# A fused graph-network kernel: the dense second layer with its residual folded into the weights, its sum copied by ScalarE and its roots taken by ScalarE and VectorE

## The chip, the cores and the metric

The kernel runs on one core of one Trainium2 chip. The metric is the device time of one execution in microseconds. The engines are TensorE (PE for its matmuls, PEld for its weight loads), VectorE (DVE), ScalarE (ACT), GpSimd (POOL) and SyncE (SP), which issues the large DMAs.

## The reference

Four graph-network layers run one after the other over the same 50,000 nodes of 128 features and 12,500 edges. Each is followed by a residual and a normalisation per row. The layer that matters here is the second (L1):

```python
def _L1_gnn_ref(x, edge_index, W):
    deg = jax.ops.segment_sum(ones(E), row, num_segments=n_nodes)
    inv_sqrt = jax.lax.rsqrt(deg + 1.0)
    xs = x * inv_sqrt[:, None]
    agg = jax.ops.segment_sum(xs[col], row, num_segments=n_nodes) + xs
    out = agg * inv_sqrt[:, None]
    return jnp.matmul(out, W.T)
# around it: x2 = normalise(x1 + L1(x1)), with mean and variance over the 128 features of a row
# normalise(v) = (v - mean(v)) / sqrt(var(v) + 1e-5)
```

A node without an edge has degree 0, so for it the layer is just `x1 @ W.T`, and its new row is `normalise(x1 @ W.T + x1)`.

## The kernel before

The kernel is one program of stages that follow each other, with a barrier between them. `second_layer()` is the stage that changes. It does two things side by side:

- **The dense part** treats all nodes as if they had no edge. The nodes are cut into 98 groups (`NG`) of 512 rows, each held as a tile of 128 x 512 (four blocks of 128 x 128, `spans`). Two groups form a pair `d` (49 pairs, `NPR`), which shares the small operations on 8 numbers per partition.
- **The edge part** computes the rows of nodes that do have edges, in 25 groups (`EGR`) of 512 edges, from rows gathered by GpSimd's indirect DMAs. Later stages take these rows where they exist.

For a dense group g the work is: `load_dense` (SP brings x1 into `dx_flat[g % 6]`), `dense_turn` (TensorE transposes it into PSUM `DT`, which is one buffer), `dense_copy` (ScalarE copies `DT` to `dxT[g % 2]`), `dense_output` (TensorE multiplies by `WL1` into `DY[g % 2]`), `dense_residual` (VectorE adds x1 and writes `dr_flat[g % 6]`), `dense_stats` and `dense_moments` (VectorE, mean and variance). Per pair follow `dense_eps` (VectorE adds 1e-5 to 8 variances), `dense_power` (GpSimd raises them to -0.5), `dense_shift` (VectorE), and then per group `dense_normalise` (ScalarE, four activations with a scale and a bias per partition) and `store_dense`.

For an edge group the work is `gather_peer` and `gather_own` (GpSimd), `scale_peer` (VectorE, L2461), `turn_peer` (TensorE, L2359), `scale_own` (ScalarE, L2409), `turn_own` (TensorE), `segment_sums`, `add_own` (VectorE), `output` (TensorE), `residual`, `stats`, `moments`, `eps` (VectorE), `power` (GpSimd), `shift` (VectorE) and `normalise` (ScalarE, L2417).

The order on each engine is written out by hand. Each engine runs a loop over k, where one turn of k (a step, from here on) takes one edge group and four dense groups. An engine executes its instructions strictly in this order and waits on semaphores (`after(engine, semaphore, g)` waits until event g has happened). TensorE's step is:

```python
for k in range(EGR + 1):
    dense(2 * k)                      # turn(4k), output(4k-1), turn(4k+1), output(4k)
    staged(k, EGR, turn_peer)
    staged(k - 1, EGR, turn_own)
    dense(2 * k + 1)                  # turn(4k+2), output(4k+1), turn(4k+3), output(4k+2)
    staged(k - 1, EGR, output)
```

So the dense groups that come after `turn_peer` in this order wait for the peer's scaled rows, whether they need them or not.

## Time and profile before

| what | value |
|---|---|
| median of 3 runs | 4410.17 us (4407.81 to 4410.22) |
| the profiled execution's own time | 4406.22 us |
| its span in the trace | 4404.2 us |
| `second_layer` in the trace | about 1439 to 1835 us |
| busy in that stretch of 396 us | DVE 335.6, POOL 308.8, ACT 273.8, PE 240.0 us |
| granted TensorE clock there | 0.80 of full |
| DMA | 0.67 of the 16 engines, 197 GB/s |

The stage is 9% of the span, and the change touches nothing outside it. "Busy" is the time in which an engine has an instruction running. An engine with a high busy share is not necessarily the one that sets the time. For this the waits are needed. A granted clock of 0.50 is TensorE's lower level, 1.2 GHz, and 1.00 the upper one, 2.4 GHz.

### The profile page before, as it was taken

Reading aid. Unit: us, or ns where it says so; the run is one execution under the profiler, and the core shown is the slowest. Engines: PE = TensorE matmul, PEld = TensorE weight load, DVE = VectorE, ACT = ScalarE, POOL = GpSimd, SP = SyncE. Lnnn points to the kernel's source line nnn. Section 1 sums busy time; section 2 is a strip of 40 time slices with the busy share of each in tenths; the row PEclk is TensorE's granted clock in tenths of the full one; section 3 lists DMA queues with packets and bytes.
Section 4 is the critical chain, followed back from the end, with each engine's and each line's share of the span. In section 5 each row is a group of like instructions: output and inputs, shape, how many; then the busy total and the mean of one; then the engine's idle time right before and its main releaser. Section 6 shows DMA issues by size and latency. Waiting matters only on the chain. (4 is left out here: it accounts for less than half of the span.)

```text
span 4404.2 us, 59487 instructions
## 1 busy us (share of the span) xinstructions
PE 3497.0 (79%) x14981; PEld 2181.8 (50%) x14981; DVE 3360.6 (76%) x10477; ACT 2304.7 (52%) x4672; POOL 3043.6 (69%) x2666
## 2 busy tenths in 40 slices
PE   5688888747776566499979999999699678687984
PEld 3466666624444566444435555555344367564331
DVE  6888888846666788655647888888688689787985
ACT  2498888713344577523337777777233222132752
POOL 1378888757775788677737888888577567463547
PEclk9999999979999788799989999999899889898997
DMA  3254445433332677444433443443344278694873
GB/s 86 92 146 140 138 142 148 124 98 91 96 96 75 187 203 207 143 131 143 137 116 105 133 132 125 133 132 116 106 129 133 77 233 253 142 194 132 278 235 119
DMA packets 463646, 621.80 MB, mean 141 GB/s; under 512 B 71541, under 2 KB 220204, under 8 KB 463308
## 3 DMA queue, kind: packets, MB, share of 16 engines
q1 hardware_dynamic: 402700, 534.09, 38.6%
q0 software_dynamic: 54912, 83.37, 9.0%
q8 instruction: 125, 2.05, 0.2%
q14 instruction: 213, 1.74, 0.1%
q10 hardware_dynamic: 5696, 0.55, 0.1%
HBM read 402.95 MB, written 218.46 MB: 141 GB/s over the span
## 5 line engine op out<-in xcount | busy, mean ns | idle before, releaser
L1195 PE MATMUL ps<-big,Whh 128*128 128x512 f32 x1176 | 537.4, 593 | 0.5 <-ACT big L1400 0.5
L1615 PE MATMUL ps<-big,We 128*128 128x512 f32 x800 | 355.5, 598 | 8.4 <-DVE big L1765 4.5
L1195 PEld LDWEIGHTS ps<-big,Whh 128*128 128x128 f32 x1176 | 212.9, 191 | 214.2 <-issue 211.4
L1228 POOL TENSOR_TENSOR big<-big 128x512 f32<-128x512 f32 x196 | 248.0, 1285 | 71.5 <-ACT big L1222 71.5
L604 POOL DMA_INDIRECT me<-node_tab,ix x208 | 239.7, 1152 | 70.8 <-issue 48.3
L611 POOL DMA_INDIRECT meta<-me,rank_ix x208 | 223.4, 1074 | 63.1 <-issue 60.5
L1765 DVE SCALAR_TENSOR_TENSOR big<-r2N,zN 128x512 f32<-128x512 f32 x400 | 254.0, 686 | 9.9 <-ACT zN L1676 6.2
L1213 DVE SCALAR_TENSOR_TENSOR big<-ps,bhh,hid 128x512 f32<-128x512 f32 x196 | 146.4, 747 | 141.2 <-ACT hid L1206 137.4
L1615 PEld LDWEIGHTS ps<-big,We 128*128 128x128 f32 x800 | 150.8, 191 | 195.1 <-issue 188.7
L688 PE MATMUL ps<-big,hotrow 128*128 128x256 f32 x832 | 201.5, 398 | 22.5 <-ACT hotrow L746 12.1
L1238 POOL TENSOR_TENSOR big<-big 128x512 f32<-128x512 f32 x98 | 141.5, 1464 | 109.1 <-DVE big L1233 109.1
L2729 POOL DMA_INDIRECT xN<-x_tab,ix x100 | 167.1, 1671 | 62.1 <-PE ps L2743 30.1
L1205 ACT ACTIVATE hid<-ps,brz 128x512 f32<-128x512 f32 x196 | 134.8, 688 | 135.2 <-PE ps L1195 129.9
L700 PE MATMUL ps<-agg,W2a 128*128 128x512 f32 x392 | 193.4, 617 | 8.8 <-ACT hid L724 4.6
L688 PEld LDWEIGHTS ps<-big,hotrow 128*128 128x128 f32 x832 | 164.7, 201 | 61.0 <-issue 23.5
L637 POOL TENSOR_TENSOR rsq<-veq,mhalf 128x4 f32<-128x4 f32 x98 | 104.6, 1067 | 127.5 <-DVE veq L921 125.6
L2759 PEld LDWEIGHTS ps<-big,hid 128*128 128x128 f32 x1600 | 186.1, 194 | 8.7 <-DVE hid L2878 3.5
L2759 PE MATMUL ps<-big,hid 128*128 128x128 f32 x1600 | 188.8, 277 | 1.2 <-DVE hid L2878 1.2
L1704 ACT ACTIVATE win<-hid 128x512 f32<-128x512 f32 x50 | 31.5, 630 | 294.6 <-DVE hid L1783 294.6
L2729 POOL DMA_INDIRECT xN<-d_tab,ix x100 | 141.0, 1410 | 64.0 <-PE ps L2743 36.1
L2806 ACT ACTIVATE big<-ps 128x512 f32<-128x512 f32 x50 | 29.9, 597 | 288.6 <-PE ps L2759 288.6
L2431 ACT ACTIVATE hid<-big,shq,rsq 128x128 f32<-128x128 f32 x392 | 160.4, 482 | 32.7 <-DVE shq L2538 32.6
(421 smaller groups left out, 11045.9 us busy)
## 6 DMA issues: line engine op xcount, KB each, us to landing
xN<-x_tab SPq DMA_DIRECT2D x196, 256.0 KB, 3.3
h_tab<-yN SPq DMA_DIRECT2D x124, 256.0 KB, 2.4
krow<-key_row SPq DMA_DIRECT2D x100, 256.5 KB, 4.4
agg<-in_xt SPq DMA_DIRECT2D x98, 256.0 KB, 3.3
big<-x_tab SPq DMA_DIRECT2D x98, 256.0 KB, 3.1
x_tab<-hid SPq DMA_DIRECT2D x98, 256.0 KB, 3.5
agg<-x_tab SPq DMA_DIRECT2D x98, 256.0 KB, 2.8
x_tab<-zN SPq DMA_DIRECT2D x98, 256.0 KB, 2.0
```

Source lines behind the costliest of these rows:

```text
L604: nc.gpsimd.indirect_dma_start(me[:, t, f:f + 4], None, node_tab, at_index(which, i, j)).then_inc(noted[i % 2].sem, 16)
L611: nc.gpsimd.indirect_dma_start(meta[k], bass.IndirectOffsetOnAxis(ap=rank_ix[:, k, t:t + 1], axis=0), me[:, t, :], None).then_inc(stored[k ...
L688: last = nc.tensor.matmul(LOOK[j // 2][:, (j % 2) * LO:(j % 2 + 1) * LO], hotrow[k][:, h, j * P:(j + 1) * P], R[:, k, h, :], start=(h == 0 ...
L700: nc.tensor.matmul(HB[h][:, :], W2a[:, 0, h * P:(h + 1) * P], xt[g % 4], start=True, stop=True).then_inc(hidd, 1)
L1195: last = nc.tensor.matmul(bank[:, :], Whh[:, l, c * D:(c + 1) * D], h, start=True, stop=not both)
L1213: nc.vector.scalar_tensor_tensor(self.n[u], A[u][:, :], bhh[:, self.l, 2:3], self.rz[u][:, 0, :], ADD, MUL).then_inc(first, 1)
L1228: nc.gpsimd.tensor_tensor(self.d[u], h[u], self.n[u], SUB).then_inc(self.dd, 1)
L1615: last = nc.tensor.matmul(MS[:, :], We[:, l * NTYPE + t, :], masked[g % 2][:, t, :], start=(t == 0), stop=(t == NTYPE - 1))
L1765: last = nc.vector.scalar_tensor_tensor(masked[u][:, t, :], types[u], float(t), hs[u], EQ, MUL)
L2431: last = nc.scalar.activation(dx2_flat[g % 8][:, spans[j]], dr_flat[g % 6][:, spans[j]], ACT.Identity, scale=rsq[d % 2][:, c:c + 1], bias= ...
L2729: nc.gpsimd.indirect_dma_start(xg[u][:, j, :], None, x3_tab if l == 0 else d1_tab, at_index(IX_SRC if l == 0 else IX_SLOT, g + EDGE0, j)). ...
L2759: last = nc.tensor.matmul(OUT[u][:, spans[j]], ranked[u][m][:, spans[j]], weightI[l][m], start=(m == 0), stop=(m == TOP - 1))
```

## The change

Four things are done in `second_layer()`:

1. `with_own = WL1 + identity` is built once by VectorE in a free buffer. `dense_output` multiplies by it, so the product already holds x1 @ W.T + x1.
2. `dense_residual` on VectorE goes. `dense_evict` on ScalarE copies `DY` to `dr_flat`.
3. `dense_power` on GpSimd goes. `dense_root` on ScalarE takes the square root of the 8 values of a pair, and `dense_inverse` on VectorE takes the reciprocal and refines it with one Newton step: four small operations, each waiting for the one before it.
4. `load_dense(g)` waits for the transposes of group g - 6 and no longer for its residual, since x1's tile is not read after the transposes.

The diff:

```diff
@@ -2247,6 +2247,7 @@
             ph = Phase()
             (same_d, scale_d, peer_t, scan_d, own_d, own_t, sum_d, out_d, res_d, st_d, mv_d, eps_d, rstd_d, shift_d, x2_d) = ph.sems(15)
             dt_d, dc_d, dy_d, dr_d, ds_d, dm_d, de_d, dp_d, dh_d, dx_d = ph.sems(10)
+            root_d, guess_d, square_d, error_d, mixed = ph.sems(5)
             keys_in, x2_out, dense_in, dense_out = ph.sems(2), ph.sems(2), ph.sems(6), ph.sems(8)
             peer_in, own_in = gat_a, gat_b
             per = 16 * J
@@ -2267,6 +2268,9 @@
             dx2_flat = [hid2[q][u][:, h, :] for q in range(2) for u in range(2) for h in range(2)]
             d_stats = norm_bufs[1][0]
             NPR = NG // 2
+            with_own = hotrow[0][:, 1, 0:P]
+            d_root = [hotrow[0][:, 0, 8 * u:8 * u + 8] for u in range(2)]
+            d_error = [hotrow[1][:, 0, 8 * u:8 * u + 8] for u in range(2)]
 
             def both(t):
                 return t[:, :].rearrange("p (a j) -> p a j", a=2)
@@ -2293,7 +2297,7 @@
                         sp.dma_start(x2_rows(1, g + EDGE0), x2[g % 2][:, :, :]).then_inc(x2_out[g % 2], 16)
 
                     def load_dense(g):
-                        after(sp, dr_d, g - 6)
+                        after(sp, dt_d, g - 6)
                         sp.dma_start(dx_flat[g % 6], group(x1_tab, g)).then_inc(dense_in[g % 6], 16)
 
                     def store_dense(g):
@@ -2336,19 +2340,11 @@
                         after(pool, eps_d, g)
                         nc.gpsimd.tensor_tensor(rs[g % 2][:, :, 0], ve[g % 2][:, :, 0], mhalf[:, 0:J], ALU.pow).then_inc(rstd_d, 1)
 
-                    def dense_power(d):
-                        after(pool, de_d, d)
-                        after(pool, dh_d, d - 2)
-                        after(pool, dx_d, 2 * (d - 2) + 1)
-                        nc.gpsimd.tensor_tensor(rsq[d % 2][:, :], veq[d % 2][:, :], mhalf[:, 0:2 * J], ALU.pow).then_inc(dp_d, 1)
-
                     gather_peer(0)
                     for k in range(EGR + 4):
                         staged(k + 1, EGR, gather_peer)
-                        staged(2 * k - 1, NPR, dense_power)
                         staged(k, EGR, gather_own)
                         staged(k - 2, EGR, power)
-                        staged(2 * k, NPR, dense_power)
 
                 @block.tensor
                 def _(pe):
@@ -2381,10 +2377,12 @@
                         last.then_inc(dt_d, 1)
 
                     def dense_output(g):
+                        if g == 0:
+                            pe.wait_ge(mixed, 1)
                         after(pe, dc_d, g)
                         after(pe, dr_d, g - 2)
                         for j in range(J):
-                            last = nc.tensor.matmul(DY[g % 2][:, spans[j]], dxT[g % 2][:, spans[j]], WL1[:, :], start=True, stop=True)
+                            last = nc.tensor.matmul(DY[g % 2][:, spans[j]], dxT[g % 2][:, spans[j]], with_own, start=True, stop=True)
                         last.then_inc(dy_d, 1)
 
                     def dense(d):
@@ -2422,6 +2420,16 @@
                         after(act, dy_d, g - 2)
                         nc.scalar.activation(dxT[g % 2], DT[:, :], ACT.Copy).then_inc(dc_d, 1)
 
+                    def dense_evict(g):
+                        after(act, dy_d, g)
+                        after(act, dx_d, g - 6)
+                        nc.scalar.activation(dr_flat[g % 6], DY[g % 2][:, :], ACT.Copy).then_inc(dr_d, 1)
+
+                    def dense_root(d):
+                        after(act, de_d, d)
+                        after(act, guess_d, d - 2)
+                        nc.scalar.activation(d_root[d % 2], veq[d % 2][:, :], ACT.Sqrt).then_inc(root_d, 1)
+
                     def dense_normalise(g):
                         d, a = divmod(g, 2)
                         after(act, dh_d, d)
@@ -2435,7 +2443,9 @@
                     def dense(d):
                         for n in range(2):
                             staged(2 * d + n, NG, dense_copy)
+                            staged(2 * d + n - 1, NG, dense_evict)
                             staged(2 * (d - 2) + n, NG, dense_normalise)
+                        staged(d - 1, NPR, dense_root)
 
                     for k in range(EGR + 3):
                         staged(k - 1, EGR, scale_own)
@@ -2445,6 +2455,7 @@
 
                 @block.vector
                 def _(dve):
+                    nc.vector.tensor_tensor(with_own, WL1[:, :], ident[:, :], ADD).then_inc(mixed, 1)
                     nc.vector.memset(agg[1][:, 0, :], 0.0).then_inc(scan_d, 1)
 
                     def same_key(g):
@@ -2507,11 +2518,6 @@
                         after(dve, x2_d, g - 2)
                         nc.vector.scalar_tensor_tensor(sh[u][:, :, 0], mv[u][:, :, 0], -1.0, rs[u][:, :, 0], MUL, MUL).then_inc(shift_d, 1)
 
-                    def dense_residual(g):
-                        after(dve, dy_d, g)
-                        after(dve, dx_d, g - 6)
-                        nc.vector.tensor_tensor(dr_flat[g % 6], DY[g % 2][:, :], dx_flat[g % 6], ADD).then_inc(dr_d, 1)
-
                     def dense_stats(g):
                         after(dve, dr_d, g)
                         after(dve, dm_d, g - 2)
@@ -2532,20 +2538,32 @@
                         after(dve, dp_d, d - 2)
                         nc.vector.tensor_scalar(both(veq[d % 2]), moment(d)[:, :, :, 1], EPS, None, ADD).then_inc(de_d, 1)
 
+                    def dense_inverse(d):
+                        y, t, v = rsq[d % 2][:, :], d_error[d % 2], veq[d % 2][:, :]
+                        after(dve, root_d, d)
+                        after(dve, dh_d, d - 2)
+                        after(dve, dx_d, 2 * (d - 2) + 1)
+                        nc.vector.reciprocal(y, d_root[d % 2]).then_inc(guess_d, 1)
+                        after(dve, guess_d, d)
+                        nc.vector.tensor_tensor(t, y, y, MUL).then_inc(square_d, 1)
+                        after(dve, square_d, d)
+                        nc.vector.scalar_tensor_tensor(t, t, -0.5, v, MUL, MUL).then_inc(error_d, 1)
+                        after(dve, error_d, d)
+                        nc.vector.scalar_tensor_tensor(y, t, 1.5, y, ADD, MUL).then_inc(dp_d, 1)
+
                     def dense_shift(d):
                         after(dve, dp_d, d)
                         after(dve, dx_d, 2 * (d - 2) + 1)
                         nc.vector.scalar_tensor_tensor(both(shq[d % 2]), moment(d)[:, :, :, 0], -1.0, both(rsq[d % 2]), MUL, MUL).then_inc(dh_d, 1)
 
                     def dense_second(d):
+                        staged(d - 2, NPR, dense_inverse)
                         staged(d - 2, NPR, dense_shift)
-                        staged(2 * d - 1, NG, dense_residual)
                         staged(2 * d - 1, NG, dense_stats)
                         staged(2 * d - 1, NG, dense_moments)
                         staged(d - 1, NPR, dense_eps)
 
                     def dense_first(d):
-                        staged(2 * d, NG, dense_residual)
                         staged(2 * d, NG, dense_stats)
                         staged(2 * d, NG, dense_moments)
```

The order in which two engines now run a step, from the steady part of the stage. On ScalarE, from `scale_own` (r2N) to the edge group's `normalise` (zN), before. L2423 is `dense_copy`, and L2431 is `dense_normalise`.

```order
L2409 ACTIVATE r2N<-xN,inv_e 128x128 x4
L2423 ACTIVATE big<-ps 128x512
L2431 ACTIVATE hid<-big,shq,rsq 128x128 x4
L2423 ACTIVATE big<-ps 128x512
L2431 ACTIVATE hid<-big,shq,rsq 128x128 x4
L2417 ACTIVATE zN<-rN,shift,rstd 128x128 x4
```

The same piece of the changed kernel, whose line numbers are its own. L2421 is `dense_copy`, L2426 `dense_evict`, L2439 `dense_normalise`, L2431 `dense_root`.

```order
L2407 ACTIVATE r2N<-xN,inv_e 128x128 x4
L2421 ACTIVATE big<-ps 128x512
L2426 ACTIVATE big<-ps 128x512
L2439 ACTIVATE hid<-big,shq,rsq 128x128 x4
L2421 ACTIVATE big<-ps 128x512
L2426 ACTIVATE big<-ps 128x512
L2439 ACTIVATE hid<-big,shq,rsq 128x128 x4
L2431 ACTIVATE hotrow<-veq 128x8
L2415 ACTIVATE zN<-rN,shift,rstd 128x128 x4
```

Each dense group brings one more activation of 128 x 512, placed ahead of a `dense_normalise` of an older group, and each pair one root at the end of its half of the step. The evicted group is one behind the copied one.

On VectorE, from `scale_peer` (yN) to the statistics of dense group 4k+1, before. L2513 is `dense_residual`, L2538 `dense_shift`, L2519 `dense_stats`.

```order
L2461 TENSOR_SCALAR yN<-xN,inv_e 128x128 x4
L2513 TENSOR_TENSOR big<-ps,big 128x512
L2519 BN_STATS stats<-big 128x6 x4
L2527 BN_AGGR mvq<-stats 128x2 x4
L2496 BN_AGGR moments<-stats 128x2 x4
L2477 TENSOR_TENSOR xT<-ps,agg 128x512
L2502 TENSOR_SCALAR vareps<-moments 128x4
L2538 SCALAR_TENSOR_TENSOR shq<-mvq,rsq 128x8
L2513 TENSOR_TENSOR big<-ps,big 128x512
L2519 BN_STATS stats<-big 128x6 x4
```

The same piece of the changed kernel. L2546 to L2552 are `dense_inverse`, L2557 is `dense_shift`, L2525 `dense_stats`.

```order
L2472 TENSOR_SCALAR yN<-xN,inv_e 128x128 x4
L2525 BN_STATS stats<-big 128x6 x4
L2533 BN_AGGR mvq<-stats 128x2 x4
L2507 BN_AGGR moments<-stats 128x2 x4
L2488 TENSOR_TENSOR xT<-ps,agg 128x512
L2513 TENSOR_SCALAR vareps<-moments 128x4
L2546 RECIPROCAL rsq<-hotrow 128x8
L2548 TENSOR_TENSOR hotrow<-rsq 128x8
L2550 SCALAR_TENSOR_TENSOR hotrow<-hotrow,veq 128x8
L2552 SCALAR_TENSOR_TENSOR rsq<-hotrow,rsq 128x8
L2557 SCALAR_TENSOR_TENSOR shq<-mvq,rsq 128x8
L2525 BN_STATS stats<-big 128x6 x4
```

The two residuals are gone from this half of the step, and four dependent small operations stand ahead of `dense_shift`.

## Rows read from the trace of the kernel before

**Rows 1.** The page: the span of the profiled execution

```profile
span 4404.2 us, 59487 instructions
```

**Rows 2.** Lines of the whole program: busy us, mean ns, idle before

```profile
L2343 POOL TENSOR_TENSOR rsq<-veq,mhalf 128x8 f32<-128x8 f32 x49 | 81.4, 1661 | 20.4 <-DVE veq L2533 19.7
L2513 DVE TENSOR_TENSOR big<-ps,big 128x512 f32<-128x512 f32 x98 | 66.7, 680 | 34.1 <-PE ps L2387 34.1
```

**Rows 3.** Windows: 100 us of the layer, busy by engine, clock, DMA

```profile
core 0: us, PE busy (x) PEld busy (x) DVE busy (x) ACT busy (x) POOL busy (x), PEclk, DMA share, GB/s
1600.00:1700.00 100.00, 65.40 (x435) 63.14 (x433) 86.93 (x393) 71.86 (x182) 81.58 (x72) 0.82 0.70 204
```

**Rows 4.** Waits from 1470 to 1810 us: total us, times, longest

```profile
PE ps L2359 <- DVE yN L2461: 85.3, 22, 5.0
ACT big L2423 <- PE ps L2380: 54.1, 30, 2.5
...
DVE big L2513 <- PE ps L2387: 28.7, 21, 1.7
```

**Rows 5.** Timeline, VectorE and TensorE: start us, duration us

```profile
1603.88 0.69 DVE L2513 TENSOR_TENSOR big<-ps,big 128x512 f32<-128x512 f32 x1 [1.72 <-PE ps L2387]
...
1606.81 1.06 PE L2387 MATMUL ps<-WL,big 128*128 128x128 f32 x8
...
1610.65 0.87 DVE L2519 BATCH_NORM_STATS2 stats<-big 128x6 f32<-128x128 f32 x4
...
1614.92 1.11 PE L2359 MATMUL ps<-ident,yN 128*128 128x128 f32 x4 [4.74 <-DVE yN L2461]
...
1619.02 0.69 DVE L2513 TENSOR_TENSOR big<-ps,big 128x512 f32<-128x512 f32 x1 [1.25 <-PE ps L2387]
```

**Rows 6.** Timeline, ScalarE alone, the same step

```profile
1604.73 0.60 ACT L2423 ACTIVATE big<-ps 128x512 f32<-128x512 f32 x1 [0.43 <-PE ps L2380]
1605.23 1.63 ACT L2431 ACTIVATE hid<-big,shq,rsq 128x128 f32<-128x128 f32 x4
1606.77 1.26 ACT L2409 ACTIVATE r2N<-xN,inv_e 128x128 f32<-128x128 f32 x4
1607.93 0.58 ACT L2423 ACTIVATE big<-ps 128x512 f32<-128x512 f32 x1
```

**Rows 7.** Timeline, TensorE alone: layer's peer transposes, one product

```profile
1464.88 1.11 PE L2359 MATMUL ps<-ident,yN 128*128 128x128 f32 x4 [3.66 <-DVE yN L2461]
...
1494.23 0.66 PE L2359 MATMUL ps<-ident,yN 128*128 128x128 f32 x4 [3.33 <-DVE yN L2461]
...
1537.76 1.11 PE L2359 MATMUL ps<-ident,yN 128*128 128x128 f32 x4 [3.06 <-DVE yN L2461]
...
1599.32 1.11 PE L2359 MATMUL ps<-ident,yN 128*128 128x128 f32 x4 [4.35 <-DVE yN L2461]
...
1601.93 1.92 PE L2387 MATMUL ps<-WL,big 128*128 128x128 f32 x8
...
1814.75 1.12 PE L2359 MATMUL ps<-ident,yN 128*128 128x128 f32 x4 [4.84 <-DVE yN L2461]
```

**Rows 8.** Windows of half a microsecond, columns as in rows 3

```profile
1614.40:1614.90 0.50, 0.00 (x0) 0.00 (x0) 0.50 (x4) 0.50 (x3) 0.50 (x1) 1.00 1.09 365
...
1615.40:1615.90 0.50, 0.50 (x4) 0.50 (x4) 0.47 (x4) 0.00 (x0) 0.50 (x1) 0.50 0.00 0
```

**Rows 9.** Last stage: timeline of a root and Newton step

```profile
4255.27 0.17 DVE L3184 RECIPROCAL rsq<-veq 128x4 f32<-128x4 f32 x1
...
4256.06 0.16 DVE L3226 SCALAR_TENSOR_TENSOR shift<-moments,rstd 128x4 f32<-128x4 f32 x1
...
4257.67 0.20 ACT L3163 ACTIVATE veq<-vareps 128x4 f32<-128x4 f32 x1 [3.88 <-DVE vareps L3220]
...
4257.78 1.49 ACT L3171 ACTIVATE zN<-ps,shift,rstd 128x128 f32<-128x128 f32 x4
```

**Rows 10.** Lines of the whole program, ScalarE alone: table load

```profile
L3163 ACT ACT_TABLE_LOAD x1 | 1.3, 1283 | 2.5 <-PEq L3009 2.5
```

## The prediction

> **What bounds the stage now.** The span of the profiled execution is 4404.2 us [rows 1], and the change can only move the 396 us of the second layer. I read first the busy shares there, to see whether one engine is full: in 100 us of its steady part VectorE is busy 86.9, GpSimd 81.6, ScalarE 71.9 and TensorE 65.4 us, at a mean granted clock of 0.82 and a DMA share of 0.70 [rows 3]. None is full, so I read the waits. TensorE waits 85.3 us in 22 steps for the peer's scaled rows (`scale_peer`), ScalarE 54.1 us for the transposes behind them, and VectorE 28.7 us for the product that `dense_residual` reads, once a step and in 21 steps [rows 4]. The reader is to see one loop in these three waits, not three separate ones.
>
> The timeline shows it. From VectorE's residual at 1603.88 to the next one that had to wait, at 1619.02, is one step of 15.14 us [rows 5]. It has three pieces. VectorE works from the residual to the statistics of group 4k+3, 6.77 us (1603.88 to 1610.65). Then statistics, the edge group's residual and statistics and `scale_peer`, 4.27 us up to the start of the peer's transposes at 1614.92. Then TensorE does three sets of transposes and one dense product, 4.10 us, and releases the residual at 1619.02. All of it is a chain, since TensorE's order puts group 4k+1 behind `turn_peer`. The mean step is (1814.75 - 1464.88) / 23 = 15.21 us, over 24 starts of `turn_peer` [rows 7].
>
> The third piece depends on TensorE's clock. Ahead of `turn_peer` the engine has stood idle for 4.74 us; the half microsecond before its start is still listed at 1.00, and half a microsecond after it the clock is at 0.50, the lower of its levels (1.2 GHz) [rows 5, 8]. Four transposes then take 1.11 us where they take 0.66 at the upper level, and a product 1.92 where it takes 1.06 [rows 5, 7]. If the clock comes back within the piece it is 4.10 us, if not 1603.88 - 1599.32 = 4.56 [rows 5, 7], and the steps alternate between the two. Three sets of transposes and a product laid end to end are 5.25 us at the lower level, of which 4.56 passed, so with the same overlap 3.04 at the upper one (3 x 0.66 + 1.06) would be about 2.6 us.
>
> **The change part by part.** *VectorE* loses four residuals of 0.68 us a step [rows 2], 2.7 us, and gains two inverses. From the reciprocal to the shift behind the fourth operation is 0.79 us in the last stage [rows 9]; its tiles have 4 numbers and not 8, which I take at the same price (bounds: nothing for the extra numbers, and 2 x 0.3 us a step if each operation grew by 0.07). VectorE's work was 15.14 - 1.25 of waiting = 13.89 us [rows 5] and becomes 13.9 - 2.7 + 1.6 = 12.8.
>
> *GpSimd* loses two powers of 1.66 us a step [rows 2]. Its share was 81.6% with its queue work on top, so gathers come earlier, but the waits show no one who ends late for it, and I count nothing.
>
> *ScalarE* has per group a copy (0.50 us to the next start), a normalise (1.54) and, per step, one `scale_own` (1.16) [rows 6] and one edge normalise that I price as a dense one (1.54). An evict is an activation of the same form as the copy, 0.50. A root delays what follows by 4257.78 - 4257.67 = 0.11 [rows 9]. Sum: 4 x (0.50 + 0.50 + 1.54) + 1.16 + 1.54 + 2 x 0.11 = 13.1 us, from 10.9. It becomes the fullest engine, and no wait fits under 13.1.
>
> The Trainium skill, "ScalarE: Activation LUTs" (Rules for kernel authors), speaks against this part: simple adds and the like belong on VectorE, since it is faster per element. Here the trace differs for fp32 from PSUM: 0.58 us for a copy on ScalarE [rows 6] against 0.68 for the sum on VectorE [rows 2]. By the page the moved 512 columns should cost more than they cost before; by the rows the work shrinks by 0.1 us and what counts is where it stands in the loop.
>
> *The loop* therefore changes its first piece. After the product of group 4k+1 come now, on ScalarE: evict(4k+1), normalise, copy, evict, normalise, root, `scale_own`, copy, and evict(4k+3), which VectorE's statistics wait for. That is 0.50 + 1.54 + 0.50 + 0.50 + 1.54 + 0.11 + 1.16 + 0.50 + 0.60 = 6.95 us in place of VectorE's 6.77. VectorE is not late in it: it needs some 6.1 us in the same piece, with one inverse in it. The second piece holds no residual that is removed (4.27 stays). So at equal clock a step grows by 0.18 us: 6.95 + 4.27 = 11.22, plus 4.10 or 4.56, gives 15.32 or 15.78, mean 15.55. Saving 1.1 us of VectorE's work and 3.3 of GpSimd's buys nothing here.
>
> *The clock* is what I think decides. The last dense product ahead of TensorE's long idle stretch needs copy(4k+4). It started 1607.93 - 1603.88 = 4.05 us after the residual [rows 5, 6]. Now it starts 0.50 + 1.54 + 0.50 + 0.50 + 1.54 + 0.11 + 1.16 = 5.85 us after the evict, because two evicts and a root stand before it. The 4.74 us idle stretch shrinks by 1.8, less the 0.2 by which the loop grows, to about 3.1 us, and the rest goes to a shorter one in front of that copy. Of the 24 waits in front of `turn_peer`, all of 3.59 us or more were followed by transposes at the lower level. Five were shorter, and two of them were followed by transposes at or near the upper level, one after 3.33 us; one of 3.06 was not [rows 7]. So I take 2 of 5 steps with a fast third piece. Such a step is 11.22 + 2.6 = 13.8 us, still above the 13.1 of ScalarE. Mean step: 0.4 x 13.8 + 0.6 x 15.55 = 14.85, that is 0.36 less than 15.21. Over 24 steps -8.6 us.
>
> The Trainium skill, "TensorE: Matmul & The Clock Gate" (HAM oscillation), says that idle gaps send the engine back to half rate and names this as a cost of kernels that wait between bursts. The trace agrees with the direction after every wait from 3.59 us up, as said; for gaps of 3.1 us our rows are mixed.
>
> *Once only:* the first root needs ScalarE's table of square roots. A load is 1.28 us and there was one for all 25 roots of the last stage, though Identity activations stand between them [rows 10], so it isn't paid per root. I add 1.3 us. The Trainium skill, the same ScalarE page (What ACT_TABLE_LOAD costs), gives 2.66 us with a drain; by it the sum would be 1.4 us higher. `with_own` is built while VectorE waits for the first loads; if nothing hid it, it would be 0.3 us. The earlier `load_dense` costs nothing and helps nothing, since no transposes in the steady part wait for a load. SP issues the same DMAs in the same order.
>
> **Sum.** -8.6 + 1.3 = -7.3 us, against the profiled execution's own 4406.2 gives 4398.9. The median of the runs shown is 4.0 us above that execution, so I say 4403.
>
> **The rivals.** A difference of 0.2%, 8.8 us, is about what a measurement of this kernel can tell from none.
>
> *The clock stays as it was* (a wait that takes the place of the one removed). ScalarE's chain replaces VectorE's and the steps alternate as before: +0.18 x 24 + 1.3 = +5.6 us, 4416. For it: one gap of 3.06 us was followed by the lower clock. Against: the stretch is shorter than any of the 19 that did so always.
>
> *The clock stays low through every third piece*, the rival on the other side. If TensorE is idle twice a step and is low at each `turn_peer` without recovering in it, each step is 15.78: +0.57 x 24 + 1.3 = +15 us, 4425. It decides from a mean step of about 15.5 us upward. For it: half the steps of before are so. Against: a loop that drifts against the clock's changes has not to stay at the worst place.
>
> *ScalarE or VectorE binds and nothing else*, TensorE being at the upper level at every `turn_peer`: 13.8 a step, -1.4 x 24 + 1.3 = -33 us, 4378. For it: both gaps are below 3.59 us. Against: 3.06 at 1537.76.
>
> *The change doesn't do what it says*: an inverse that waits for its root would put VectorE late. Root(2k-1) is queued behind two normalises, but in front of the edge group's; VectorE comes to the inverse 2.1 us after `scale_peer`, when the root is done by some 2 us. Queued behind the waiting inverse would be the statistics of group 4k+1, and TensorE's next product after that. I see no price here, or at most 0.3 us a step, which the range covers.
>
> **How the numbers follow.** Mixed clock, step 14.5 to 15.2: 0.42, half of it faster than 0.2% (below 14.8) and half not. Clock as before: 0.22, within 0.2% but for a little. All fast or nearly: 0.19, faster. All low, or an unpriced wait of the new handshakes: 0.17, slower but for a little. Together 0.42 faster, 0.41 same, 0.17 slower. The range: 4384 (a mean step of 14.2) to 4422 (15.65).
>
> **What would show it.** In the trace after: ScalarE's busy share in the steady 100 us at 84 to 90; VectorE's evicted statistics waiting for ScalarE twice a step, near 0.8 and 1.5 us; TensorE's wait in front of `turn_peer` at 2.8 to 3.4 us in place of 4.7, with another of about 2.2 ahead of a dense transpose; granted clock in 1600 to 1700 above 0.82; steps of two kinds, near 13.8 and 15.5; one table load at the stage's start. I am wrong if the wait in front of `turn_peer` is still above 3.6, if ScalarE waits for VectorE's inverse, or if a step has a new wait on a DMA now that everything asks for 0.70 x 15.2 / 14.85 = 0.72 of the DMA engines.

## The result, and the profile after

| kernel | median us | range | ratio to before, 95% interval |
|---|---|---|---|
| before | 4409.09 | 4407.81 to 4410.22 | |
| after | 4375.27 | 4371.66 to 4376.82 | 0.9922 [0.9905, 0.9939] |

The changed kernel is 33.8 us faster. The forecast was 4403, with a range down to 4384, so the result lies below it. It lies 3 us from the rival "ScalarE or VectorE binds and nothing else" (4378). Run twice more on other occasions, the changed kernel took 4378.82 (0.9932) and 4382.05 us (0.9938).

The windows of the changed kernel answer to [rows 3]; the last is the whole layer.

```profile
core 0: us, PE busy (x) PEld busy (x) DVE busy (x) ACT busy (x) POOL busy (x), PEclk, DMA share, GB/s
1500.00:1600.00 100.00, 63.39 (x435) 59.58 (x434) 84.37 (x445) 90.48 (x235) 62.85 (x63) 0.86 0.71 217
1600.00:1700.00 100.00, 62.40 (x482) 57.49 (x480) 89.43 (x479) 96.19 (x249) 66.12 (x66) 0.95 0.73 230
...
1439.00:1835.00 396.00, 218.98 (x1592) 200.75 (x1592) 309.44 (x1613) 328.80 (x842) 240.55 (x241) 0.87 0.67 204
```

ScalarE went from 71.9 to 96.2 us in the 100, and the mean granted clock from 0.82 to 0.95. Nearly full is now one engine, where no engine was by this count before. The waits from 1470 to 1780 us answer to [rows 4].

```profile
PE ps L2355 <- DVE yN L2472: 61.8, 22, 3.2
POOL rstd L2341 <- DVE vareps L2513: 60.6, 22, 6.1
PE ps L2376 <- ACT big L2421: 59.1, 43, 2.3
...
DVE stats L2525 <- ACT big L2426: 23.7, 30, 1.5
```

TensorE's longest wait ahead of the peer's transposes (L2355) is 3.2 us and no longer 5.0, and there is a second one of up to 2.3 ahead of a dense group's transposes (L2376). The timeline shows one step, to be set against [rows 5, 6].

```profile
1601.00 0.19 DVE L2546 RECIPROCAL rsq<-hotrow 128x8 f32<-128x8 f32 x1
...
1601.51 0.60 ACT L2426 ACTIVATE big<-ps 128x512 f32<-128x512 f32 x1
...
1601.84 0.17 DVE L2557 SCALAR_TENSOR_TENSOR shq<-mvq,rsq 128x8 f32<-128x8 f32 x1
...
1607.83 0.58 ACT L2426 ACTIVATE big<-ps 128x512 f32<-128x512 f32 x1
...
1608.07 1.08 PE L2376 MATMUL ps<-ident,big 128*128 128x128 f32 x4 [2.25 <-ACT big L2421]
...
1608.44 0.87 DVE L2525 BATCH_NORM_STATS2 stats<-big 128x6 f32<-128x128 f32 x4 [0.79 <-ACT big L2426]
...
1608.95 1.92 PE L2385 MATMUL ps<-hotrow,big 128*128 128x128 f32 x8
...
1610.90 0.60 ACT L2426 ACTIVATE big<-ps 128x512 f32<-128x512 f32 x1 [0.47 <-PE ps L2385]
...
1612.76 0.66 PE L2355 MATMUL ps<-ident,yN 128*128 128x128 f32 x4 [1.90 <-DVE yN L2472]
...
1614.13 1.06 PE L2385 MATMUL ps<-hotrow,big 128*128 128x128 f32 x8
...
1615.22 0.60 ACT L2426 ACTIVATE big<-ps 128x512 f32<-128x512 f32 x1
```

The reader is to see two things. The evict of group 4k+1 (L2426) stands at 1601.51 and, 13.71 us later, at 1615.22: this is the step, and ScalarE waits in it only once, for 0.47 us. And TensorE still drops to its lower level (1.08 us for four transposes at 1608.07, 1.92 for the product behind them), but now behind the wait of 2.25 us for ScalarE's copy. By the time of the peer's transposes it is back at the upper level (0.66 and 1.06). Windows of half a microsecond, as in [rows 8], say the same.

```profile
1608.20:1608.70 0.50, 0.50 (x3) 0.50 (x4) 0.26 (x2) 0.50 (x3) 0.50 (x1) 0.50 1.17 300
...
1613.20:1613.70 0.50, 0.50 (x8) 0.50 (x6) 0.47 (x5) 0.50 (x2) 0.00 (x0) 1.00 0.62 213
```

The starts of the peer's transposes, as in [rows 7], with the dense product behind four of them (a few of the 25 starts; the 23 from 1483.62 on are at most 3.18 us behind the work before them):

```profile
1457.00 0.99 PE L2355 MATMUL ps<-ident,yN 128*128 128x128 f32 x4
...
1483.62 0.66 PE L2355 MATMUL ps<-ident,yN 128*128 128x128 f32 x4 [3.10 <-DVE yN L2472]
...
1526.04 1.88 PE L2385 MATMUL ps<-hotrow,big 128*128 128x128 f32 x8
...
1539.12 0.66 PE L2355 MATMUL ps<-ident,yN 128*128 128x128 f32 x4 [3.12 <-DVE yN L2472]
...
1541.21 1.91 PE L2385 MATMUL ps<-hotrow,big 128*128 128x128 f32 x8
...
1554.32 1.12 PE L2355 MATMUL ps<-ident,yN 128*128 128x128 f32 x4 [2.10 <-DVE yN L2472]
...
1556.94 1.92 PE L2385 MATMUL ps<-hotrow,big 128*128 128x128 f32 x8
...
1570.05 0.79 PE L2355 MATMUL ps<-ident,yN 128*128 128x128 f32 x4 [3.12 <-DVE yN L2472]
...
1572.34 1.78 PE L2385 MATMUL ps<-hotrow,big 128*128 128x128 f32 x8
...
1585.32 0.66 PE L2355 MATMUL ps<-ident,yN 128*128 128x128 f32 x4 [1.85 <-DVE yN L2472]
...
1790.84 0.66 PE L2355 MATMUL ps<-ident,yN 128*128 128x128 f32 x4 [3.12 <-DVE yN L2472]
```

Of the 23 starts, 21 are at the upper level. That is not yet 21 fast third pieces: behind the starts at 1524.67 (0.65 us, not shown) and 1539.12 the clock falls within the piece, and the product takes 1.88 and 1.91 us. Of the 22 steps from 1483.62 on, the product of the third piece is at the upper level in 18, and these take 13.65 to 13.80 us. The other four take 14.45, 15.20, 15.73 and 15.27, about 6 us more than four steps of 13.7. Waits of 3.1 us stand behind a dense product at the upper level, waits of 1.9 behind one at the lower, which ends later. The mean step is (1790.84 - 1457.00) / 24 = 13.91 us, its rhythm 13.70 (1497.28 - 1483.62 = 13.66, 1612.76 - 1599.05 = 13.71).

**Where the 33.8 us lie.** I cut each profiled execution in three: all that stands ahead of the layer's first peer transposes, the layer from there to ScalarE's first instruction of the next stage, and everything behind it. Before: 1453.4, 399.4 and 2551.4 us. After: 1457.0, 371.3 and 2541.6. The layer of the two repeats takes 371.5 and 371.0, with 2549.9 and 2546.9 behind. So the layer is 28 us shorter each time. The stages behind it, which the change doesn't touch, scatter by 8 us between executions of one kernel. Some 6 of the 33.8 us are not the layer's. Against the kernel before beside them, the repeats are 32.2 (4410.99 - 4378.82) and 27.5 us (4409.58 - 4382.05) faster, so the medians too scatter by some 6.

### The profile page after: what moved, and what is told of

It reads as the page before. It is cut to its first block and busy times, and to the rows that moved or that the text cites. A ratio compares the mean times of both kernels' runs of the same rounds, so it can differ in the third digit from the quotient of the medians.

```text
span 4369.9 us, 59733 instructions
## 1 busy us (share of the span) xinstructions
PE 3468.0 (79%) x14981; PEld 2147.0 (49%) x14981; DVE 3328.8 (76%) x10576; ACT 2359.3 (54%) x4820; POOL 2934.2 (67%) x2617
## 5 line engine op out<-in xcount | busy, mean ns | idle before, releaser
L2747 POOL DMA_INDIRECT xN<-x_tab,ix x100 | 157.2, 1572 | 68.5 <-PE ps L2761 36.8
L707 PE MATMUL ps<-W2b,hid 128*128 128x128 f32 x1056 | 140.5, 290 | 43.6 <-DVE rN L902 31.1
L3056 POOL TENSOR_TENSOR rstd<-vareps,mhalf 128x4 f32<-128x4 f32 x98 | 98.7, 1007 | 106.3 <-DVE vareps L3108 106.3
```

What stands on the lines that cost most here:

```text
L2747: nc.gpsimd.indirect_dma_start(xg[u][:, j, :], None, x3_tab if l == 0 else d1_tab, at_index(IX_SRC if l == 0 else IX_SLOT, g + EDGE0, j)). ...
```

## The experiments

The filler transposes in four of them write to a bank that is then overwritten, so they add work and change no result. "Start" means the start of the peer's transposes; 0.66 us or less is the upper level, 1.06 to 1.12 the lower, and between them the clock changed within the four. "Layer" is the time just defined, of one profiled execution.

| kernel | median us (range) | before beside it | ratio, interval | layer |
|---|---|---|---|---|
| e1_roots_only | 4435.43 (4433.76 to 4437.81) | 4410.05 | 1.0059 [1.0042, 1.0076] | 425.3 |
| e2_evict_only | 4400.88 (4388.47 to 4411.06) | 4410.05 | 0.9977 [0.9958, 0.9995] | 394.7 |
| e3_before_filled | 4397.29 (4392.24 to 4401.62) | 4410.05 | 0.9965 [0.9954, 0.9977] | 383.4 |
| e4_early_copy | 4414.74 (4406.39 to 4419.91) | 4410.05 | 1.0011 [1.0002, 1.0021] | 402.4 |
| e9_after_again | 4378.82 (4377.11 to 4382.81) | 4410.99 | 0.9932 [0.9915, 0.9949] | 371.5 |
| e10_early_copy_filled | 4385.65 (4385.03 to 4392.49) | 4410.99 | 0.9951 [0.9932, 0.9969] | 374.7 |
| e11_evict_filled | 4392.22 (4388.67 to 4411.28) | 4410.99 | 0.9967 [0.9953, 0.998] | 379.5 |
| e12_after_reordered | 4376.75 (4375.36 to 4381.52) | 4410.99 | 0.9929 [0.9911, 0.9946] | 362.7 |
| e13_late_load_again | 4379.51 (4370.49 to 4384.16) | 4409.58 | 0.9928 [0.9914, 0.9941] | 378.0 |
| e14_reordered_again | 4373.44 (4366.96 to 4375.72) | 4409.58 | 0.9912 [0.9896, 0.9927] | 362.4 |
| e15_after_third | 4382.05 (4376.04 to 4385.16) | 4409.58 | 0.9938 [0.9925, 0.9951] | 371.0 |

### Each part alone

**Roots alone.** The changed kernel with the residual and the plain weights back, and the old wait of the load; against before only the roots differ. The lines that place them in the orders of three engines:

```diff
-                        staged(2 * k - 1, NPR, dense_power)
@@
-                        staged(2 * k, NPR, dense_power)
@@
+                        staged(d - 1, NPR, dense_root)
@@
+                        staged(d - 2, NPR, dense_inverse)
```

> Only the roots are moved (ScalarE's square root, VectorE's Newton step); the residual stays on VectorE and the product with the plain weights. Clock theory: the loop through the peer's transposes stays VectorE's, one inverse longer (0.8 us), the idle stretch ahead of the peer's transposes stays above 4 us and the clock low there, so a step is 15.9 to 16.4 us and the time 4426 to 4438 us. GpSimd theory (the gain comes from the two powers taken off its queue): at least 10 us faster than before, under 4399 us.

The time is as the clock theory had it, and the layer grew by 25.9 us. VectorE is busy 91.5 us in the 100 from 1600, and all six starts there are at the lower level after waits of 4.92 to 5.65 us. The mean step is (1847.54 - 1472.81) / 23 = 16.29 us. Freeing GpSimd buys nothing while VectorE's chain is the loop, and makes TensorE's wait longer.

**Evict alone.** The changed kernel with the powers back on GpSimd and without root and inverse. Against before, beside the weights and the wait of the load, this differs (lines of two engines' blocks):

```diff
+                    def dense_evict(g):
+                        after(act, dy_d, g)
+                        after(act, dx_d, g - 6)
+                        nc.scalar.activation(dr_flat[g % 6], DY[g % 2][:, :], ACT.Copy).then_inc(dr_d, 1)
@@
-                    def dense_residual(g):
```

> Only the residual is moved (identity in the weights, sum copied by ScalarE, later condition of the loads); GpSimd keeps its powers. Clock theory: the copy ahead of the idle stretch is late as in the changed kernel, but GpSimd's own queue needs 15.14 - 0.33 = 14.8 us a step (before's trace), so the step falls only to about 14.8 us, 4400 us; if the longer idle stretch lets the clock drop again, 4405 to 4412. VectorE theory (the gain is the 2.7 us of residuals taken off VectorE): nearly the whole gain, 4375 to 4385 us.

The time was as expected, the reason only in part. The steps are 13.53 us where the clock stays up in the third piece and ScalarE doesn't wait for gathered rows. Of the 14 steps from 1573.21 on, six start low and in 11 the product of the third piece takes 1.27 us or more, so that the mean is (1784.49 - 1573.21) / 14 = 15.09. Four of the starts:

```profile
1602.30 1.11 PE L2363 MATMUL ps<-ident,yN 128*128 128x128 f32 x4 [3.04 <-DVE yN L2474]
1617.50 0.66 PE L2363 MATMUL ps<-ident,yN 128*128 128x128 f32 x4 [3.12 <-DVE yN L2474]
1631.03 0.66 PE L2363 MATMUL ps<-ident,yN 128*128 128x128 f32 x4 [1.85 <-DVE yN L2474]
1645.63 1.12 PE L2363 MATMUL ps<-ident,yN 128*128 128x128 f32 x4 [1.85 <-DVE yN L2474]
```

The same wait of 1.85 us is followed by either level. The wait just ahead does not decide the level by itself. Alone the parts give +25.4 and -9.2 us by medians, together -34; in the layer +25.9 and -4.7, together -28.1.

### The clock

**Fillers in the kernel before**, ahead of the peer's transposes:

```diff
+                    def keep_busy(g):
+                        after(pe, res_d, g - 2)
+                        after(pe, sum_d, g - 2)
+                        for _ in range(8):
+                            nc.tensor.transpose(TO[:, spans[0]], ident[:, :], ident[:, :])
+
                     for k in range(EGR + 1):
                         dense(2 * k)
+                        staged(k, EGR, keep_busy)
                         staged(k, EGR, turn_peer)
```

> The kernel before with eight more transposes of the identity a step on TensorE, into a bank that is overwritten right after, placed in the idle stretch ahead of the peer's transposes. Clock theory: the third piece of the loop falls from 4.1 or 4.56 to about 2.6 us, the granted clock rises, and the step goes to GpSimd's 14.8 us: 4398 to 4402 us; if GpSimd is not a bound, to VectorE's 13.9: 4378 us. A theory without the clock: more work on TensorE's path, 4409 to 4415 us.

Added work makes the kernel before 12.8 us faster (16.0 in the layer), as expected within 1 us: the clock of 1600 to 1700 is 0.90 in place of 0.82. The mean step is (1763.89 - 1488.83) / 19 = 14.48 us, and what ends last has changed. ScalarE's waits from 1470 to 1780 us, of which the first two are 10.0 and 2.6 us in the kernel before:

```profile
ACT r2N L2416 <- DMA xN<-x_tab,ix: 26.0, 12, 3.0
ACT r2N L2416 <- DMA big<-x_tab,ix: 19.7, 7, 4.2
ACT big L2430 <- PE ps L2380: 18.9, 20, 2.2
```

ScalarE now waits 45.7 us for rows gathered by GpSimd's DMAs. VectorE, busy 95.2 us of the 100 from 1600, is not far from full either.

**One copy earlier in the changed kernel.** Copy(4k+4) goes ahead of `scale_own`, which brings back one long wait in place of two; the work is the same:

```diff
                         for n in range(2):
                             staged(2 * d + n, NG, dense_copy)
+                            if k is not None and n == 0:
+                                staged(k - 1, EGR, scale_own)
                             staged(2 * d + n - 1, NG, dense_evict)
@@
-                        staged(k - 1, EGR, scale_own)
-                        dense(2 * k)
+                        dense(2 * k, k)
```

> The changed kernel with one ScalarE operation moved: the first dense copy of a step stands ahead of the edge group's scaling and not behind it; everything else, the evicts' places too, is the same. Clock theory: the last product ahead of TensorE's idle stretch comes 1.2 us earlier, the stretch grows from 3.1 to 4.3 us, the clock is low at the peer's transposes and steps go back to 15.3 to 15.8 us: 4405 to 4415 us. VectorE or GpSimd theory: no work has changed, 4372 to 4378 us.

```profile
1592.85 1.11 PE L2355 MATMUL ps<-ident,yN 128*128 128x128 f32 x4 [4.29 <-DVE yN L2473]
1608.58 1.11 PE L2355 MATMUL ps<-ident,yN 128*128 128x128 f32 x4 [4.29 <-DVE yN L2473]
1623.62 1.11 PE L2355 MATMUL ps<-ident,yN 128*128 128x128 f32 x4 [4.34 <-DVE yN L2473]
```

This is the decisive run: one copy earlier by one `scale_own` takes the time back to that of before. Against the changed kernel it costs 39 us by the first medians (4414.74 - 4375.27), 33 to 36 against its repeats, and 31 in the layer (402.4 - 371.3). All 23 starts behind a wait of 4.27 us or more are low, and the steps alternate between about 15.0 and 15.73. Then the same with the eight fillers:

> The changed kernel with the early copy, which was 39 us slower, plus eight filler transposes a step in the lengthened idle stretch. Clock theory, on a chip with before near 4410: the fillers keep the clock up and the loss goes, 4370 to 4380 us. If the early copy hurt by its place in ScalarE's order and not by the clock: 4405 to 4415 us.

The forecast of 4370 to 4380 was missed by 6 us, but most of the loss comes back: 29 us by medians, and 28 of the 31 in the layer. Most steps are 13.7 us, as from 1636.95 to 1650.66, so the copy's place in ScalarE's order costs nothing where the clock is up. Eight of the 25 starts are still at 1.06 to 1.12, which fits the 3 (layer) to 7 us (median) by which it stays short of the changed kernel.

**The peer's transposes later** in the changed kernel, behind the product of group 4k+1, so that the third piece leaves the loop:

```diff
                             staged(2 * d + n - 1, NG, dense_output)
+                            if k is not None and n == 0:
+                                staged(k, EGR, turn_peer)
+                                staged(k - 1, EGR, turn_own)
@@
                         dense(2 * k)
-                        staged(k, EGR, turn_peer)
-                        staged(k - 1, EGR, turn_own)
-                        dense(2 * k + 1)
+                        dense(2 * k + 1, k)
```

> The changed kernel with the peer's and own transposes behind the product of group 4k+1. On a chip with before near 4410: loop theory 4358 to 4366 us, ScalarE's 13.1 us bind; if ScalarE was the bound already, 4373 to 4378 us.

> The changed kernel with the peer's transposes behind the product of group 4k+1, once more. In the one profile so far its layer took 362.7 us against 371.3 and 371.5 of the changed kernel, but the stages behind the layer took 2553.6 against 2541.6 and 2549.9, and the medians lay 2 us apart. If the 8.6 us in the layer are real and the rest is scatter of the later stages, the layer is at 361 to 364 us again and the median is 3 to 9 us under the changed kernel's (4367 to 4376). If ScalarE's 13.7 us a step is all that counts, the layer is at 368 to 372 and the median at 4375 to 4380.

Here the peer's transposes scarcely wait (0.25 us at most in 1590 to 1680) and none of 25 is at the lower level; ScalarE is busy 95.65 us of 100. The rhythm is 13.67 us, only 0.03 less than before the edit, and not the 13.1 of the loop theory. Within half a microsecond a step ScalarE had been the limit already; in the step from 1604.85 it still waits 0.36 us for VectorE's shift and 0.35 for a product. The low stretch has not gone. In the first of the two profiles it stands in every step from 1468.23 on, on the product behind copy(4k+4), and the mean clock is lower than in the changed kernel (0.86 against 0.95):

```profile
1600.00:1700.00 100.00, 70.92 (x470) 65.40 (x471) 89.31 (x474) 95.65 (x248) 66.17 (x67) 0.86 0.76 232
```

```profile
1600.80 1.92 PE L2385 MATMUL ps<-hotrow,big 128*128 128x128 f32 x8
...
1604.85 0.66 PE L2355 MATMUL ps<-ident,yN 128*128 128x128 f32 x4
```

In the second profile it stands there up to the step from 1707.77 and is gone from 1721.50 on, and the steps are 13.7 us with it and without it. So it is the place of the low stretch that costs here, and not its length. The layer is 8.6 us shorter all the same (362.7 and 362.4 against 371.0 to 371.5), as the mean step fell from 13.91 to (1782.67 - 1457.52) / 24 = 13.55. The difference is the four slow steps of the changed kernel, about 6 us, and its slower first two, about 2.5. The first time the medians hid it behind the scatter of the later stages (4376.75 against 4378.82); the second time it shows: 4373.44 against 4382.05, with the same 2546.9 us behind the layer in both profiles. (Those two profiled executions, 4375.68 and 4376.04 us, lie closer than the medians, since this one began its layer 8 us later.) By the layer this is the fastest version measured.

> The changed kernel itself, beside the kernel before on whatever chip this call gets. The last call's chip was slower for the kernel before too (4498 us) and showed waits there whose releaser the profile lists as remote, so its four results can't be set beside the earlier ones. If this chip is as the first ones (before near 4410): 4372 to 4379 us. If it is as the last (before near 4498): the changed kernel is slower than before, 4560 to 4620 us, since three relatives with the roots on ScalarE were.

> The changed kernel itself, beside the two others on the same chip. Both theories expect 4371 to 4383 us, a layer of 371 us and two to four slow starts of the peer's transposes; the later stages between 2541 and 2554 us show how far they scatter.

Both repeats of the changed kernel were as expected, with the layer within 0.5 us of 371.3. Each has the group of four slow steps once, as the first had, but elsewhere: 14.51, 15.26, 15.73 and 15.27 us from 1632.71 on, and 14.43, 15.18, 15.73 and 15.27 from 1619.83 on.

### GpSimd

**Evict alone, with the fillers of above:**

> The evict alone (GpSimd keeps its powers) with eight filler transposes a step. On a chip with before near 4410: if the clock alone makes the gain, 4370 to 4380 us and steps of 13.5 to 13.9; if GpSimd's powers bind on average, above 4388 us.

The mean step is (1803.55 - 1501.57) / 21 = 14.38 us, against 13.91 in the changed kernel and (1793.91 - 1510.51) / 20 = 14.17 in the early copy with fillers; neither of these has the powers. Two causes lengthen the steps here. In five of the 21 the clock is down in the third piece (its product takes 1.35 to 1.91 us). In nine others ScalarE waits for gathered rows, a wait that the changed kernel doesn't have from 1470 to 1780 us:

```profile
ACT r2N L2422 <- DMA xN<-x_tab,ix: 8.5, 7, 3.4
ACT r2N L2422 <- DMA big<-x_tab,ix: 2.2, 3, 0.9
```

The three steps from 1602.49 to 1645.00 show this cause by itself. All their dense products take 1.06 us, the upper level, and the steps take 13.93, 14.23 and 14.35 us, each 13.63 plus the wait for the rows:

```profile
1609.88 1.28 ACT L2422 ACTIVATE r2N<-xN,inv_e 128x128 f32<-128x128 f32 x4 [0.30 <-DMA xN<-x_tab,ix]
...
1624.10 1.28 ACT L2422 ACTIVATE r2N<-big,inv_e 128x128 f32<-128x128 f32 x4 [0.60 <-DMA big<-x_tab,ix]
...
1638.46 1.28 ACT L2422 ACTIVATE r2N<-xN,inv_e 128x128 f32<-128x128 f32 x4 [0.72 <-DMA xN<-x_tab,ix]
```

GpSimd, which issues these gathers, waits for others only some 5 us in 310; the rest of its gaps is "issue". In the kernel before (first fence below) it was nearly so, with 9.4 us of waits for VectorE's variances and 0.9 for its shifts:

```profile
POOL xN L2327 <- issue: 22.5, 83, 0.3
POOL xN L2333 <- issue: 14.0, 51, 0.3
POOL rsq L2343 <- DVE veq L2533: 9.4, 16, 0.8
POOL big L2333 <- issue: 7.4, 27, 0.3
```

```profile
POOL xN L2331 <- issue: 21.4, 78, 0.3
POOL xN L2337 <- issue: 14.1, 51, 0.3
POOL big L2337 <- issue: 6.9, 25, 0.3
```

Before, these gaps are (22.5 + 14.0 + 7.4) / 3.1 = 14.2 us in 100, on top of a busy share of 81.6: 95.8%, or 14.6 us of the 15.2 of a step. In the filled kernel (second fence) it is 84.6 + 13.7 = 98.3% of 14.38, 14.1 us. So with the powers GpSimd has a floor of about 14.1 to 14.6 us a step, an estimate that takes the "issue" gaps as work; single steps are shorter (13.52 us), so it is a floor for the mean. Without two powers of 1.66 [rows 2] it would be near 11, and it waits 60.6 us for others in the profile after.

### The earlier load

```diff
                     def load_dense(g):
-                        after(sp, dt_d, g - 6)
+                        after(sp, dr_d, g - 6)
```

> The changed kernel with the old wait of the load (for the evict of group g - 6 and not for its transposes). If the earlier load counts nothing, as the prediction had it, the time is that of the changed kernel, 4371 to 4383 us, with steps of 13.70 us and no wait of the dense transposes or of ScalarE for a load. If the earlier load is what keeps the loads clear of the gathers and stores, ScalarE's evict or TensorE's dense transposes wait once or more a step and the time is above 4390 us.

4379.51 us beside 4382.05 of the changed kernel: the earlier load is worth nothing that the medians can tell. The layer of its one profile is 6.5 to 7 us longer. Two stretches of low starts (from 1496.58 and from 1721.62) fell in it; nothing waits for a load among its largest waits. Whether the later load has a part in those stretches, one profile doesn't show.

### Four runs on another chip

These ran on a chip on which the kernel before itself took 4497.73 us, and can't be set beside the others. The first, second and fourth are the kernels of e11, e10 and e12, the third that of e13; what they were to show was read from those:

> The kernel with the evict alone (GpSimd keeps its powers) and eight filler transposes a step in the idle stretch ahead of the peer's transposes. If the clock alone makes the gain, the steps become 13.5 to 13.9 us throughout, as the fast ones of the evict-only trace are (13.53 us), and the time 4370 to 4378 us, so that the roots contribute nothing but an undisturbed rhythm. If GpSimd's powers bind on average, steps stay at 14.4 us or more and the time above 4388 us.

> The changed kernel with the early copy, which was 39 us slower, plus eight filler transposes a step in the lengthened idle stretch. Clock theory: the fillers keep the clock up and the whole loss goes: 4370 to 4380 us. If the early copy hurt by its place in ScalarE's order and not by the clock: 4405 to 4415 us as without fillers.

> The changed kernel with the old condition of the loads: a dense tile is loaded once the residual's successor, the evict, of six groups before is done, not its transposes. No transposes of the steady part wait for a load, so by my reading nothing changes: 4372 to 4379 us. If the earlier loads are part of the gain: 4385 us or more.

> The changed kernel with TensorE's order changed: the peer's and own transposes stand behind the product of group 4k+1 and not ahead of it. Loop theory: the dense groups no longer wait for the edge rows, the third piece of the loop goes, and ScalarE's 13.1 us bind: 4358 to 4366 us. If ScalarE was the bound already: 4373 to 4378 us; if the edge part's later transposes make VectorE's add wait: above 4380 us.

They took 4507.43 (1.0021 [1.0005, 1.0036]), 4600.95 (1.0229 [1.018, 1.0278]), 4615.96 (1.0264 [1.0239, 1.0288]) and 4564.63 us (1.0154 [1.0123, 1.0184]). So there the three with the roots on ScalarE lose 103, 118 and 67 us. ScalarE's evict has a wait in them, listed as "remote", that no run on the other chips has: from 1440 to 1960 us once in the first, and 21, 16 and 17 times in the others. One of the late load:

```profile
1718.89 0.60 ACT L2426 ACTIVATE big<-ps 128x512 f32<-128x512 f32 x1 [4.88 <-remote]
```

The product that this evict reads had long ended, and the profile names no instruction of this core as the releaser. The same four kernels gain on the other chips, so these runs say nothing of the clock's part. But they bound the result: the gain is shown on chips that run the kernel before in 4409 to 4411 us, and on this one the changed kernel's nearest relative, which differs from it only in the load's wait, loses 118 us. Why that chip is slower, and why the evict waits there, stays open. The changed kernel itself wasn't run on it, so whether it would lose there too is not shown.

## Why the prediction was wrong

**Right: the loop and its pieces.** From the evict of 4k+1 to the end of that of 4k+3 I gave 6.95 us; it is 1608.41 - 1601.51 = 6.90. The second piece, given as 4.27, is 1612.76 - 1608.44 = 4.32. The third at the upper level, given as 2.6, is 1615.22 - 1612.76 = 2.46. The inverse, given as 0.79, is 1601.84 - 1601.00 = 0.84. ScalarE's work, given as 13.1, is 13.71 - 0.47 = 13.24. The step without a low third piece, given as 13.8, is 13.70.

**Right: what the clock does and which edit moves it.** The wait ahead of the peer's transposes shrank from 4.74 to 3.1 us and a second one of 2.25 appeared, as forecast, because evicts and root stand before copy(4k+4). The early copy shows this link: it moves one copy and adds no work, brings back the long wait and takes back the gain, and its fillers return most of it. The Trainium skill, "TensorE: Matmul & The Clock Gate" (HAM oscillation), names idle gaps between bursts as the cause of half rate. The runs agree from 3.59 us up, where all starts of the kernel before, of the roots alone and of the early copy are low; between 1.8 and 3.2 us the runs show both levels.

**Wrong: the term "I take 2 of 5 steps with a fast third piece".** Measured were 18 of 22 (21 of 23 by the starts alone). The 2 of 5 came from five short waits in the trace before, which stood in a loop with another rhythm. Three of the five were waits of 0.46 to 0.67 us, and two of these were followed by the lower level (1.12 us both), so the sample spoke against its own use.

I treated the wait just ahead as what sets the level. But the evict alone has both levels behind 1.85 us, and in the changed kernel 2.25 us was followed by low transposes and 1.90, in the same step, by transposes at the upper level. What differs is where in the step the low stretch falls. Before, it began at the peer's transposes, on the loop's path. Now it falls, where there is one, on the transposes and product behind copy(4k+4). Of that only 0.47 us reaches ScalarE, and the peer's rows come from VectorE anyway. In 14 of the 22 steps no dense product is low at all, and in four more only the one behind copy(4k+4) is. Why the clock stays up through the third piece in 18 steps, and not in the others, is not settled.

From the second start on, as 15.21 was taken before, the mean step is (1790.84 - 1468.70) / 23 = 14.01 us in place of the assumed 14.85. With it the sum gives (14.01 - 15.21) x 24 + 1.3 = -27.5, against the -28.1 measured in the layer. The lower end of the range does not follow from its own sum: a mean step of 14.2 gives (14.2 - 15.21) x 24 + 1.3 + 4406.2 + 4.0 = 4387, and 4384 is near what comes out without the 4.0, which the upper end has. The result lies below both.

**Wrong: "I count nothing" for GpSimd.** This did no harm to the sum only because the sum had the clock low in most steps. With the clock up, the powers would have held the mean step above 14, as both filled kernels show (14.48 and 14.38, with ScalarE waiting 45.7 and 10.7 us for gathered rows). With the evict on ScalarE that is 4392.22 against 4378.82 by medians, 13 us, and 379.5 against 371.3 in the layer, 8 us; part of it is the clock of the five slow pieces, and the changed kernel with fillers, which would part the two, wasn't run. The rival at 4378 was right only because GpSimd's relief was in the change too. The premise "the waits show no one who ends late for it" was not right either: in the kernel before, ScalarE waits 12.6 us for gathered rows. And it is not enough to ask whether others wait for GpSimd; it must be asked whether GpSimd itself ever waits.

**The other parts.** The table load is 1.28 us once in the layer, at 1461.38, and the root behind it starts 0.02 us after its end, so no second term for a drain shows. By the medians the earlier load counts nothing. The inverse waits for no root. ScalarE's share is above the forecast 84 to 90 only since the step is shorter. The evict takes 589 ns on ScalarE against 680 for the sum on VectorE [rows 2]. The Trainium skill, "ScalarE: Activation LUTs" (Rules for kernel authors), gives additions to VectorE as the faster engine per element, with its figure for bf16. These two rows don't test that rule, as the prediction took them to: the evict is a copy, the addition went into TensorE's weights, and no run has one operation on both engines. What counted is that the engine that took the tile over had room.

**The chances.** All-fast had 0.19 and the range stopped at 4384. Both ends of the unknown share, none and all, should have been inside it, as the rows for waits near 3.1 us excluded neither.

## What to carry to other kernels

Where TensorE's clock falls on the path of a loop, ask where in the step the low stretch will be after an edit, not how long the wait ahead of it is. And count the low stretches in the piece itself: here two starts at the upper level stood ahead of a low product. Samples from the old rhythm don't carry over, so a share of fast steps is to be ranged from none to all. Test whether an engine is full by its own waits: GpSimd, whose only gaps were "issue", was full at a busy share of 84.6. And look at two parts together when each frees a different engine; here one lost 26 us in the layer and one gained 5, and both together gained 28.

## What the runs showed of the hardware

Eight extra transposes a step made the kernel before 12.8 us faster, and one copy issued earlier made the layer of the changed kernel 31 us longer (33 to 39 by medians), both through the granted clock. With the peer's transposes later, a low product of 1.92 us in every step cost nothing (a rhythm of 13.67 us at a mean clock of 0.86). A spread of 8 us between executions of one kernel, in stages that no edit touches, can hide or feign a gain of that size; the time of the layer alone, cut from the trace, was steady within 0.5 us for three executions of the changed kernel. One chip ran the kernel before in 4497.73 us, where the others took 4409 to 4411, and there relatives of the changed kernel were 67 to 118 us slower than it.
